# Reciprocal square roots of the layer norms: one power operation on GpSimd in place of a seed and three Newton steps on VectorE

## What is computed

```python
def _layernorm(x, axis=-1, eps=1e-05):
    m = jnp.mean(x, axis=axis, keepdims=True)
    v = jnp.var(x, axis=axis, keepdims=True)
    return (x - m) / jnp.sqrt(v + eps)

# attention part, on xn = _layernorm(x)
a = jnp.tanh(xn @ WA.T);  b = xn @ WB.T            # 16 states
g = sigmoid(xn @ Wg.T + bg);  dx = xn @ WD.T + bD
h_t = a_t * h_{t-1} + b_t                          # along the sequence
x = x + (hs @ WC.T) * g + dx * (1 - g)

# expert part, on h2 = _layernorm(x)
shared = silu(h2 @ shared_gate_w) * (h2 @ shared_up_w) @ shared_down_w
probs = softmax(h2 @ router_w);  top 2 of 16 experts per token
x = x + shared + sum over the two of prob * (silu(h2 @ g) * (h2 @ u)) @ d
```

## Time and profile before

| what | value |
|---|---|
| time, median of 3 runs (range) | 772.59 us (772.11 to 775.65) |
| span of the profiled execution | 772.7 us |
| PE busy | 601.8 us (78%) |
| DVE busy | 539.9 us (70%), 1660 instructions |
| ACT busy | 321.6 us (42%) |
| POOL busy | 368.3 us (48%) |
| half steps 0 to 14, one | some 22.8 to 23.8 us |

### The profile page before, as it was taken

How to read it: one execution, slowest core, us unless ns; L and a number is a source line. 1 busy time by engine, 2 the same in 40 slices (tenths; PEclk the granted TensorE clock), 3 DMA queues, 4 the chain that set the end, 5 groups by cost and what they waited for, 6 DMA issues and landing times.

```text
span 772.7 us, 16380 instructions
## 1 busy us (share of the span) xinstructions
PE 601.8 (78%) x3710; PEld 499.9 (65%) x3741; DVE 539.9 (70%) x1660; ACT 321.6 (42%) x733; POOL 368.3 (48%) x516
## 2 busy tenths in 40 slices
PE   3689899999999999999974788988988988970000
PEld 2467777777778777778763677877877877750000
DVE  8778898888899988897866245545445444545776
ACT  4366455565555565555452233333333333330000
POOL 3214445654545644445647356556556656661000
PEclk9789999999999999999997699999999999995555
DMA  4994111110101111101114434434544444417998
GB/s 155 275 330 125 38 40 50 56 48 34 48 34 56 55 41 41 48 34 57 57 45 171 117 120 156 155 114 155 156 131 148 146 135 146 147 50 247 379 385 293
DMA packets 82806, 96.91 MB, mean 125 GB/s; under 512 B 10142, under 2 KB 74066, under 8 KB 82774
## 3 DMA queue, kind: packets, MB, share of 16 engines
q1 hardware_dynamic: 61270, 54.32, 23.3%
q0 software_dynamic: 13056, 33.84, 12.1%
q10 hardware_dynamic: 8448, 8.39, 3.1%
HBM read 52.04 MB, written 46.57 MB: 128 GB/s over the span
## 4 chain that ended last, share of the span: by engine, by line
PE 57%; issue 12%; DVE 9%; DMA 7%; ACT 3%; POOL 2%; SPq 1%; DVEq 1%; POOLq 0%; ACTq 0%
PE gd L600 14%; PE tr L398 8%; PE gu L405 5%; DMA raw_w<-expert_results 5%; PE tr L405 5%; PE gd L436 5%; PE dn L405 5%; PE gu L617 4%; PE dn L617 4%; PE cb L398 3%; PE misc L405 2%; PE misc L527 2%; DVE tokens L1293 1%; SPq L383 1%; DMA expert_rows<-row_buf,slot 1%
## 5 line engine op out<-in xcount | busy, mean ns | idle before, releaser
L1355 POOL DMA_INDIRECT expert_rows<-row_buf,slot x128 | 132.0, 1031 | 145.3 <-DVE slot L1011 107.2
L1423 POOL DMA_INDIRECT expert_results<-raw_w,row_ids x144 | 141.6, 983 | 67.9 <-issue 35.2
L600 PE MATMUL gd<-w_hi,bx 128*128 x576 | 112.0, 297 | 0.6 <-DVE bx L1235 0.6
L436 PE MATMUL gd<-wgd,xT 128*128 128x512 f32 x384 | 103.0, 405 | 4.6 <-DVE xT L936 4.6
L398 PE MATMUL tr<-ident,row_buf 128*128 128x128 f32 x416 | 64.6, 279 | 46.4 <-issue 32.9
L1235 DVE TENSOR_TENSOR bx<-tr,bx 128x512 fp32r<-128x512 f32 x72 | 49.8, 692 | 71.6 <-ACT bx L820 63.7
L398 PEld LDWEIGHTS tr<-ident,row_buf 128*128 128x128 f32 x416 | 49.1, 142 | 64.1 <-issue 57.8
L600 PEld LDWEIGHTS gd<-w_hi,bx 128*128 128x128 f32 x576 | 85.1, 192 | 3.1 <-issue 1.0
L820 ACT ACTIVATE bx<-tr 128x512 fp32r<-128x512 f32 x71 | 42.5, 599 | 101.2 <-PE tr L398 101.2
L436 PEld LDWEIGHTS gd<-wgd,xT 128*128 128x128 f32 x384 | 71.7, 196 | 18.9 <-DVE xT L936 3.1
L1254 DVE TENSOR_TENSOR raw_w<-gd,raw_w 128x256 f32<-128x256 f32 x72 | 30.6, 425 | 64.7 <-ACT raw_w L826 64.7
(11 more groups left out here) (155 smaller groups left out, 1250.0 us busy)
## 6 DMA issues: line engine op xcount, KB each, us to landing
row_buf<-expert_rows SPq DMA_DIRECT2D x144, 130.0 KB, 2.1
raw_w<-expert_results SPq DMA_DIRECT2D x32, 512.0 KB, 10.9
tokens<-in_x SPq DMA_DIRECT2D x16, 512.0 KB, 4.9
out<-tokens ACTq DMA_DIRECT2D x16, 512.0 KB, 7.1
expert_results<-raw_w,row_ids POOLq DMA_INDIRECT x144, 2.4
expert_rows<-fill_rows SPq DMA_DIRECT2D x17, 130.0 KB, 2.6
raw_w<-in_gate_w SPq DMA_DIRECT2D x16, 128.0 KB, 4.3
raw_w<-in_up_w SPq DMA_DIRECT2D x16, 128.0 KB, 4.4
```

The source lines that it names most:

```text
L436: pe.matmul(gd[j % 2][:], xT[a][:, c, j * P:(j + 1) * P], wgd[b][:, c, :], start=(a, b, c) == (0, 0, 0), stop=False)
L600: last = pe.matmul(bgu[p][:, h * 2 * F:(h + 1) * 2 * F], bx[a][:, p, (h * KC + c) * P:(h * KC + c + 1) * P], gate_up_w[b][:, bass.ds(at[h] ...
L1355: pool.indirect_dma_start(out=rows, out_offset=bass.IndirectOffsetOnAxis(ap=slot[:, q, choice, j:j + 1], axis=0), in_=row_buf[:, q, j, :], ...
L1423: pool.indirect_dma_start(out=results, out_offset=bass.IndirectOffsetOnAxis(ap=row_ids[:, at, h:h + 1], axis=0), in_=y[:, w, h, :], in_off ...
```

## The change

The chain of 13 DVE operations becomes three operations on two engines: DVE adds eps to the variances (`spreads`), GpSimd raises the eight columns to the power -0.5 (`roots`, a `tensor_tensor` of 128x8 with operation pow, the exponents from a constant tile), and DVE makes the shifts (`shifts`). The semaphore `newton` becomes three. In a half step `spreads` stands where m = 0 stood, `shifts` stands at the head of the next half step where m = 8 stood, and `roots` stands on GpSimd between the last `x_plus_dx` and the sends that wait for `slot_ready`. The first of the roots comes after all of GpSimd's constants, the second after the low parts of the weights.

```diff
-            def newton_op(h, p, m):
-                mean, var = moments[:, p, :, 0], moments[:, p, :, 1]
-                if m >= 2:
-                    dve.wait_ge(newton, NEWTON * h + m)
...
-                ins.then_inc(newton, 1)
+            def spreads(h, p):
+                dve.tensor_scalar(spread[:], moments[:, p, :, 1], EPS, None, ALU.add).then_inc(spread_ready, 1)
+
+            def shifts(h, p):
+                dve.wait_ge(rstd_ready, h + 1)
+                dve.scalar_tensor_tensor(shift[:], moments[:, p, :, 0], -1.0, rstd[:], ALU.mult, ALU.mult).then_inc(
+                    shift_ready, 1)
...
                 if back:
-                    newton_op(s + 2, p, 8)
+                    shifts(s + 2, p)
...
-                next_newton(0)
-                next_newton(1)
+                if front:
+                    spreads(s + 3, 1 - p)
...
+            def roots(h):
+                wait_apart(pool, spread_ready, h + 1)
+                pool.tensor_tensor(rstd[:], spread[:], half_power[:], ALU.pow).then_inc(rstd_ready, 1)
+
+            link(pool.memset(half_power[:], -0.5))
...
+            roots(0)
             wait_apart(pool, ffn_hi, 3)
...
+                if isinstance(s, int) and s == -1:
+                    roots(1)
                 if front:
                     x_plus_dx(0)
...
                 if front:
                     x_plus_dx(3)
+                    roots(s + 3)
                 if back:
                     wait_apart(pool, slot_ready, k + 1)
```

More of the change, by code:

```diff
@@ L114, in preln_gated_scan_and_routed_experts @@
         shift = sb_a("shift", [P, 2 * J])
-        half_var = sb_a("half_var", [P, 2 * J])
-        newton_t = sb_a("newton_t", [P, 2 * J])
+        spread = sb_a("spread", [P, 2 * J])
+        half_power = sb_a("half_power", [P, 2 * J])
         earlier = sb_a("earlier", [P, P], BF16)
@@ L185, in preln_gated_scan_and_routed_experts @@
         ln2_moments = sem("ln2_moments")
-        newton = sem("newton")
+        spread_ready = sem("spread_ready")
+        rstd_ready = sem("rstd_ready")
+        shift_ready = sem("shift_ready")
         xn_ready = sem("xn_ready")
@@ L722, in half @@
                 if back:
-                    act.wait_ge(newton, NEWTON * (s + 3))
+                    act.wait_ge(shift_ready, s + 3)
                     if known(k, 2):
@@ L873, in ln1_means @@
                 dve.bn_aggr(moments[:, m, J + j, :], raw1[:, j, :]).then_inc(ln1_moments, 1)
-            def newton_op(h, p, m):
-                mean, var = moments[:, p, :, 0], moments[:, p, :, 1]
-                if m >= 2:
-                    dve.wait_ge(newton, NEWTON * h + m)
-                if m == 0:
-                    ins = dve.tensor_scalar(half_var[:], var, -0.5, -0.5 * EPS, ALU.mult, ALU.add)
-                elif m == 1:
-                    ins = dve.tensor_scalar(newton_t[:], var, EPS, None, ALU.add)
-                elif m == 2:
-                    ins = dve.tensor_scalar(rstd[:].bitcast(I32), newton_t[:].bitcast(I32), -0.5, RSQRT_SEED,
-                                            ALU.mult, ALU.add)
-                elif m == NEWTON - 1:
-                    ins = dve.scalar_tensor_tensor(shift[:], mean, -1.0, rstd[:], ALU.mult, ALU.mult)
-                elif m % 3 == 0:
-                    ins = dve.tensor_tensor(newton_t[:], rstd[:], rstd[:], ALU.mult)
-                elif m % 3 == 1:
-                    ins = dve.tensor_tensor(newton_t[:], newton_t[:], half_var[:], ALU.mult)
-                else:
-                    ins = dve.scalar_tensor_tensor(rstd[:], newton_t[:], 1.5, rstd[:], ALU.add, ALU.mult)
-                ins.then_inc(newton, 1)
+            def spreads(h, p):
[4 more added lines that the diff above has]
+                    shift_ready, 1)
             cnt, ntile, upto, stride = (per_expert[:, m, :] for m in range(4))
@@ L1031, in half @@
                     dve.wait_ge(xn_ready, J)
-                    for m in range(NEWTON):
-                        newton_op(1, 1, m)
-                if back:
-                    newton_op(s + 2, p, 11)
+                    spreads(1, 1)
+                    shifts(1, 1)
                 if tail:
@@ L1186, in _ @@
             dve.wait_ge(ln1_moments, J)
-            for m in range(NEWTON):
-                newton_op(0, 0, m)
+            spreads(0, 0)
+            shifts(0, 0)
             dve.wait_ge(attn_w_in, W * 9)
```

20 lines of the change are left out of this document (1 added, 19 removed).

## The result

| | before | after |
|---|---|---|
| median, us (6 runs each) | 773.55 | 778.65 |
| span of the profiled execution | 772.7 | 776.0 |
| ratio to the kernel before, 95% interval | 1 | 1.0069 [1.0043, 1.0096] |

The kernel became slower, by 5 us, where the forecast of 770.9 us said no change. The two ratios agree: 0.7 to 1%.

What follows compares the result with a forecast made beforehand. PE was taken as the bound (95% busy in the half steps), DVE mattering only where PE waits for it. Sum: 772.7 - 0.75 (half steps) - 0.8 (start) - 0.3 (end) = 770.85, 770.9 us; range 768.3 to 812 us.

Steps and rivals of the forecast that it cites:

- the list of what would make the prediction wrong: DVE idle ahead of shift, PE idle after it; a much longer first power; half steps shorter by over 0.2 us.
- D = 1.0 us: Time of GpSimd's power on eight columns, taken as 1.0 us; lower bound 0.26, upper bound 16 us.
- the rival of loaded code: GpSimd's first power loads code: 1.28 us once gives 772.2 us, 6 us by the skill near 776.9; chance 0.04.
- value by value: Rival: the power on GpSimd handles values in series, D = 7 to 16 us, total 858 to 1011 us; chance 0.13.
- D up to 2.0 us is covered: Half steps: a power up to 2.0 us delays nothing; each us beyond costs a us in each of 15.
- Half steps, -0.75 us: With D = 1.0, the 15 half steps gain 0.05 us each at their seams, 0.75 us in all.
- the prediction's signs: Signs of being right, among them DVE's busy time down by 20 us or more with half steps as long as before.
- the half steps give more: Rival: 0.2 us gained in each half step and 1.1 at the end, 766.3 us; chance of over 0.5% 0.12.
- The start, 2D - 2.8: Change at the scan of half step -1, whose second power waits behind the weights' low parts: -0.8 us at D = 1.0.
- The end, -0.3: End of part one: last h2 rows about 1.1 us earlier, sends stretched by DVE; between -1.1 and +0.2, taken as -0.3.
- The lower end of the range: 768.3 us, given as half of the larger gain, that of the rival at 766.3 us.
- 1.1 us late before row numbers come late: GpSimd's sends behind the power may start 1.1 us late without delaying row numbers and xdx, from idle time of 1.14.

Runs made afterwards that it cites:

- The two ratios: Changed kernel against the kernel before, unchanged: 1.0069 in the first measurement, 1.0096 in a second comparison on another chip.
- the second power: Changed kernel with 32 empty instructions and the power issued twice, the first into a tile nobody reads; 797.14 us, ratio to the kernel before 1.0326.
- copy of before: The kernel before, unchanged, run again for its trace on the second set's chip; median 771.40 us.
- the product: Changed kernel with 32 empty instructions and the power replaced by a product with 1.0 (root left out); third set 764.03 us, ratio to the kernel before 0.9902.

## Why the prediction was wrong, step by step

- **The missing term.** The sum priced 11 operations removed, one added and one wait, and took everything else in the program as unmoved. But every instruction ahead of the loop that goes moves the loop, by 62 places here, from three blocks to four. Shown by six placements (the changed kernel's own and 32, 96 and 128 more, the kernel before's own and 32 more): the cost, 11.2 us (779.79 to 768.55), appears and vanishes with instructions that do nothing. None of the rivals had it, nor anything on the list of what would make the prediction wrong. Its mark is on no row that I had read: the instruction queue's packets, 20 in the whole program and none in the loop.
- **D = 1.0 us.** It was 1.68, inside the bounds, outside the 0.7 to 1.3 that I had worked out from an assumed 25 to 60 steps, which no run shows. A product of that size took 0.20 us. (By the rows an operation starts in 0.26 - 32 x 0.0021 = 0.19 us, not 0.24, so one of eight columns takes 0.21, not 0.26.) The price is the same for the first call (1.68 at 7.05 us): the rival of loaded code fell, with its 1.28 us by rows and with the 6 us that the Trainium skill, GPSIMD Engine Reference, section Instruction dispatch, has for the first call of freshly loaded code. So did value by value.
- **"D up to 2.0 us is covered"** was right in mechanism, and the edge was at 1.77, an estimate from the half steps of the second power. The root got by with 0.1 us to spare, so the forecast that it costs the half steps nothing was nearer to failing than its text shows.
- **Half steps, -0.75 us.** Misread in both directions. With the loop well placed the regular half steps are as long as before (22.93 + 23.49 for 22.94 + 23.48 us), so the seams gave nothing. VectorE's busy time fell by 16.7 us in all (539.9 to 523.2), not by the 20 or more of the prediction's signs. But eight half steps of the loop took 185.2 to 185.7 us against 186.3 and 187.2 in the two traces of before. PE's waits for chosen_any from 150 to 345 us went from 3.1 us (copy of before) to 1.2. That is the rival *the half steps give more*, at about half its size, in single executions. Ahead of the loop there is more of it: half step 1 took 26.5 and 24.0 us in the two traces of before (the table ahead of the prediction has 22.8 to 23.8 us for every half step; half steps 0 and 1 are longer), and 22.8 in all three with 32 or 96 more. There GpSimd had waited 2.4 and 1.3 us for the landing of its first sends, 1.1 us with 32 more; in the first of the two traces the granted clock was 0.5 for 3.4 us besides (82.8).
- **The start, 2D - 2.8.** With D = 1.68 the formula gives +0.56 us; the scan went from 22.94 to 23.40, +0.46. The formula was right for the scan, its D was not. That the time follows the scan one to one was not: against the product, 2.9 us at the scan went with 6.7 us at misc of half step 1.
- **The end, -0.3.** From the last block's misc to the end the traces have 401.5 and 401.1 us (before) and 400.7 and 402.3 (after), 399.7, 400.5 and 400.1 with 32, 32 and 96 more. In the first trace after the change the sends of the earlier trace rows were not stretched, but GpSimd's weight subtractions behind them took 11.27 us instead of 6.94; in the second trace one of the last four sends took 5.16 us again. The term lies within that scatter.
- **The lower end of the range.** The forecast took 768.3 us for half of the larger gain; half of 6.4 us is 3.2, which gives 769.5. Nothing hung on it.
- **A row misread.** I read the 1.14 us ahead of L1371 in the earlier trace rows as a wait for PE. In the changed kernel with 32 more the same wait is 1.15 to 1.43 us in the loop and ends with the landing of the sends just before it, so the sends can't start "1.1 us late before row numbers come late"; they come late at once. Since the root let them start earlier, nothing hung on it.

With D = 1.68 in the same steps the forecast for the well-placed kernel would be 772.7 + 0.56 - 0.75 - 0.3 = 772.2 us, and it measured 3 to 4 us below the kernel before (ratios 0.9957, 0.9945, 0.9960). In the traces about 1.2 us of that is in the loop and about 1.2 at the end; half step 1 gives 1.2 us or more, and the start takes 1 to 2 back.

The best kernel found is the changed one with 32 instructions more, 768.5 us against 771.4 to 772.2 for the kernel before in the same sets. It is a gain only as long as nobody adds or removes VectorE instructions ahead of the loop.

## What to carry to other kernels

An edit that changes the number of an engine's instructions ahead of a hardware loop can make that engine fetch its loop again on every turn. Look at the instruction queues in the DMA part of the profile's page: packets during the loop, and an engine idle for "issue" at the branch, mean that the loop doesn't stay in. Compare two versions of a kernel only at equal placement, or move the loop by some idle instructions (here 32 or 96, in an idle time) before judging the edit itself.

## What was not expected of the hardware

- VectorE's code comes in packets of 8 KB, some 129 instructions apart in the trace. By the model, a loop of 279 or 320 recorded instructions stayed in where it touched three blocks of 128, and cost five packets and 2.7 to 3.1 us of waiting per turn where it touched four. The packets and the waits are measured; the blocks are worked out from six placements. The Trainium skill, Runtime: NRT & Kernel Launch, section Instruction fetch mechanics, says that a taken branch to a page outside the window of two pages of 16 KiB stalls for the fetch. If the window is the current page and the next, both loops, being longer than a page, should have stalled at each turn-back by this rule; the traces show it for one placement and not for the other, in pieces of 8 KB.
- A power of 128x8 values on GpSimd took 1.64 to 1.68 us, a product 0.20 us, the first call no longer than the rest.
- A VectorE operation of 0.17 us beside a running GpSimd subtraction of 1024 columns took until that ended, 2.35 us, and a one-input operation of 0.17 us took 1.34 us beside the same subtraction (17.63 in the changed kernel); four statistics beside it took their usual 1.39 us.
- A wait of PE of 3.07 us for VectorE was followed by 6.8 us of granted clock 0.5 (1.2 GHz) in the kernel before with 32 more, and the clock fell at three of its four turn-backs. In the changed kernel, where PE waited 1.8 to 2.0 us, it fell at one of four in each of two traces.
